# Softmax denominators summed in pairs of key tiles, shift rows by a whole-array transpose, and the batch loop written out

## Chip, cores and metric

One Trainium2 chip, one of its cores. The metric is the device time of one execution in microseconds (us): 2568.3 us as the median of three runs (2564.93 to 2572.62).

## What is computed

Cross-attention followed by a gated feed-forward block, both with a residual. The batch is 16, with 224 queries and 750 keys each, model width 512, 16 heads of 32:

```python
qh, kh, vh = proj(layernorm(x), Wq, bq), proj(ctx, Wk, bk), proj(ctx, Wv, bv)
attn = softmax(einsum('bhqd,bhkd->bhqk', qh, kh) / sqrt(32))
x = x + einsum('bhqk,bhkd->bhqd', attn, vh) @ Wo.T + bo
h = silu(fp4_linear(layernorm(x), w_gate)) * fp4_linear(layernorm(x), w_up)
x = x + fp4_linear(h, w_down)
```

`fp4_linear` rounds input and weight, in blocks of 16, to eight magnitudes with a common scale. The feed-forward width is 1408.

## The kernel before

**Stages.** `attention` runs first (to about 1797 us of the profile), then `feed_forward_weights` splits the rounded weights, then `feed_forward` runs. The change is in `attention` alone.

**Tiling.** Each batch has four slots, one for each group of four heads (`HG`); slot number and group number are the same, and `t` is the number of a group counted over all batches. The 750 keys are six tiles (`KT`) of 125 (`KW`), taken in three pairs `p`. In a slot TensorE makes twelve `score` units (pair p, head j; line 490), each of two key tiles in one bank, and ScalarE takes their exponential into `probs[p]` (line 542). A `pv` unit (line 505) multiplies one pair by the values: eight matmuls, each of 32 output columns, head j in partitions 32j to 32j+31 of `pv_bank[t % 2]`. An fp32 matmul leaves two records in the trace, so a `pv` unit has 16.

**The denominator.** GpSimd adds the six key tiles into one `prob_sum`: one add for pair 0 (line 717) and two chained ones for each of pairs 1 and 2 (line 722), five to a slot. When all five are there, TensorE multiplies the sum with a block of ones (`sum`, line 512, four matmuls, eight records) into the other half of `pv_bank`. VectorE then takes the reciprocal (657) and scales the heads (661), ScalarE and VectorE split the result (584, 665).

**The shift.** For the group one ahead, TensorE makes sixteen `max` units (475) into `max_bank`, VectorE reduces each (617), and after the eighth and the sixteenth negates the maximum into `neg_max` (622). TensorE turns these four columns into rows 96 to 99 of a bank by a matmul with the identity (`shift`, 479), ScalarE copies them into `qstack` (578), where the next group's scores take them up. `max` needs `q_masked`, which SyncE's DMA queue writes from `q_part` (803).

**Other work in the slots.** Projections of keys (429), queries (440), values (449) and the output (465) of this batch or of the one to come. VectorE also rounds a share of the feed-forward weights in slots 0, 1 and 3 (`ffn_quant`, eleven steps in lines 849 to 869; the last is line 869) and SyncE stores it (785). SyncE stacks keys and queries of the next group by DMA (`stack_low` 811, `stack` 817 and 820) and loads the context (788) and x (792) of the next batch in slot 0. GpSimd also adds the output bias to the residual in slot 3 (735).

**Order.** Nothing is planned at run time. Every unit has a place in its slot on a scale on which score i stands at i; `SLOT_PLACES` holds the places by slot, `slot_units` sorts the units by them, and each of the five engines walks through the same list and does its part of each unit, waiting on semaphores. An engine never passes over a unit. `phases` runs batch 0 as written-out code, batches 1 to 14 in one hardware loop (`engine.Fori`, in which the counts waited for are computed in registers), and batch 15 as written-out code again, followed by `END_UNITS`.

## Time and profile before

| | |
|---|---|
| median of three runs | 2568.3 us |
| the profiled execution | 2569.35 us, span of its trace 2567.3 us |
| TensorE matmul busy | 2236.7 us (87%), 15012 records |
| VectorE busy | 2028.4 us (79%) |
| ScalarE busy | 850.8 us (33%) |
| GpSimd busy | 785.2 us (31%) |
| mean granted TensorE clock | 0.93 of full speed |
| GpSimd adds of `prob_sum` (lines 717, 722) | 64 and 256, 694.7 us together |
| `sum` matmuls (line 512) | 512 records, 39.7 us |
| `shift` matmuls (line 479) | 256 records, 45.4 us |

The page's busy shares are averages over stages with different limits. Below, a batch of the loop is followed in the timeline; a row there has start, duration, engine, line, operation, output<-input, the number of merged records, and in brackets how long the engine had been idle before it and what ended the idle time. "PE" is TensorE, "DVE" VectorE, "ACT" ScalarE, "POOL" GpSimd, "SPq" SyncE's DMA queue. "Issue" is idle time that nothing in the profile explains.

### The profile page before, as it was taken

How to read it: one execution, taken by the hardware profiler on the slowest of the kernel's cores; microseconds unless marked ns; L12 is line 12 of the kernel's file. 1: busy time of each engine (PE TensorE's matmuls, PEld its weight loads, DVE VectorE, ACT ScalarE, POOL GpSimd, SP SyncE). 2: the span in 40 equal slices, each digit the busy share in tenths (PEclk: the TensorE clock that was granted, in tenths of full speed). 3: DMA queues.
4: the chain of work that ended last, by engine and by line, in shares of the span. 5: the costliest groups of instructions: out<-in, count | busy, mean ns of one | idle time of the engine just before them, and what ended most of it. 6: DMA issues, size and time to landing. Idle time of an engine off the chain costs nothing. (4 is left out here: it accounts for less than half of the span.)

```text
span 2567.3 us, 46677 instructions
## 1 busy us (share of the span) xinstructions
PE 2236.7 (87%) x15012; PEld 1846.1 (72%) x15012; DVE 2028.4 (79%) x3101; ACT 850.8 (33%) x1677; POOL 785.2 (31%) x484
## 2 busy tenths in 40 slices
PE   4989888798888889888898878887499999999998
PEld 4777667676667667676676667674378888888887
DVE  4878778787877678777787877776689999999986
ACT  3434344343434334343343434333311111111111
POOL 0444444444434434443434434445000000000000
PEclk9989899898989889988998989897799999999999
DMA  4342333433233342333433233332500101101000
GB/s 149 96 118 76 108 84 109 115 78 110 75 108 95 93 111 78 101 86 104 116 77 110 73 106 84 103 85 56 163 22 29 37 25 37 33 28 37 25 25 25
DMA packets 136288, 204.70 MB, mean 80 GB/s; under 512 B 33872, under 2 KB 84560, under 8 KB 133568
## 3 DMA queue, kind: packets, MB, share of 16 engines
q1 hardware_dynamic: 136128, 202.22, 28.1%
q8 instruction: 143, 2.34, 0.4%
q14 instruction: 17, 0.14, 0.0%
HBM read 75.67 MB, written 23.33 MB: 39 GB/s over the span
## 5 line engine op out<-in xcount | busy, mean ns | idle before, releaser
L617 DVE TENSOR_REDUCE row_max<-max_bank 112x1 f32<-112x376 f32 (+1 forms) x1024 | 524.3, 540 | 343.8 <-PE max_bank L475 338.9
L722 POOL TENSOR_TENSOR prob_sum<-prob_sum,probs 125x896 f32<-125x896 f32 x256 | 556.1, 2172 | 491.0 <-ACT probs L542 479.7
L542 ACT ACTIVATE probs<-score_bank 125x448 f32<-125x448 f32 x768 | 405.7, 543 | 379.4 <-PE score_bank L490 374.7
L475 PE MATMUL max_bank<-k_high,q_masked 128*112 128x376 f32 (+1 forms) x1024 | 349.6, 385 | 143.1 <-DVE row_max L617 71.8
L490 PE MATMUL score_bank<-qstack,kstack 100*128 100x224 f32 x1536 | 319.5, 295 | 69.7 <-issue 66.1
L490 PEld LDWEIGHTS score_bank<-qstack,kstack 100*128 100x128 f32 x1536 | 279.8, 203 | 116.7 <-issue 104.0
L475 PEld LDWEIGHTS max_bank<-k_high,q_masked 128*112 128x112 f32 x1024 | 176.5, 190 | 227.7 <-DVE row_max L617 105.0
L717 POOL TENSOR_TENSOR prob_sum<-probs 125x896 f32<-125x896 f32 x64 | 138.6, 2166 | 379.5 <-ACT probs L542 294.8
L449 PE MATMUL proj_bank<-wv_hi,ctx_hi 128*128 128x256 f32 x768 | 226.2, 294 | 4.3 <-DVE wo_lo L696 4.3
L1115 PE MATMUL gate_bank<-ffn_gate_hi,f_xqt 128*128 128x512 f32 (+1 forms) x672 | 218.8, 387 | 8.1 <-DVE f_xqt L1221 8.1
L505 PE MATMUL pv_bank<-probs,values 125*32 125x224 f32 x3072 | 221.7, 411 | 0.0
L449 PE MATMUL proj_bank<-wv_hi,ctx_lo 128*128 128x256 f32 x768 | 220.0, 286 | 0.0
L449 PE MATMUL proj_bank<-wv_lo,ctx_hi 128*128 128x256 f32 x768 | 219.5, 286 | 0.0
L1160 ACT ACTIVATE f_act_gate<-gate_bank 128x512 f32<-128x512 f32 (+1 forms) x84 | 47.3, 563 | 516.4 <-PE up_bank L1115 516.4
L1139 PE MATMUL down_bank<-ffn_down_hi,f_hqt 128*128 128x512 f32 x616 | 207.2, 403 | 6.6 <-DVE f_hqt L1237 6.6
L1115 PE MATMUL up_bank<-ffn_up_hi,f_xqt 128*128 128x512 f32 (+1 forms) x672 | 212.3, 377 | 0.0
L1179 POOL TENSOR_TENSOR f_rstd<-f_mean_var,ln_consts 128x1 f32<-128x1 f32 x28 | 5.4, 192 | 634.8 <-DVE f_mean_var L1196 634.8
L429 PE MATMUL proj_bank<-ctx_hi,wk_hi 128*128 128x376 f32 (+1 forms) x512 | 180.2, 352 | 20.0 <-DVE ctx_lo L651 20.0
L550 ACT ACTIVATE k_high<-proj_bank,biases 128x376 fp32r<-128x376 f32 (+1 forms) x128 | 73.6, 575 | 354.1 <-PE proj_bank L429 354.1
L429 PE MATMUL proj_bank<-ctx_lo,wk_hi 128*128 128x376 f32 (+1 forms) x512 | 177.4, 346 | 0.0
L429 PE MATMUL proj_bank<-ctx_hi,wk_lo 128*128 128x376 f32 (+1 forms) x512 | 175.8, 343 | 0.0
L449 PEld LDWEIGHTS proj_bank<-wv_hi,ctx_hi 128*128 128x128 f32 x768 | 150.6, 196 | 13.6 <-issue 6.1
(120 smaller groups left out, 4523.8 us busy)
## 6 DMA issues: line engine op xcount, KB each, us to landing
kstack<-k_high SPq DMA_DIRECT2D x512, 93.8 KB, 2.2
ctx_raw<-in_ctx SPq DMA_DIRECT2D x16, 1500.0 KB, 7.0
kstack<-k_low SPq DMA_DIRECT2D x256, 93.8 KB, 2.2
qstack<-q_part SPq DMA_DIRECT2D x768, 28.0 KB, 1.8
ffn_quant<-fw_share SPq DMA_DIRECT2D x48, 176.0 KB, 1.8
fw_raw<-ffn_quant SPq DMA_DIRECT2D x33, 256.0 KB, 4.1
xn<-in_x SPq DMA_DIRECT2D x16, 448.0 KB, 8.4
q_masked<-q_part SPq DMA_DIRECT2D x256, 28.0 KB, 1.8
```

Source lines behind the costliest of these rows:

```text
L429: last = nc.tensor.matmul(out[:, 0:hi - lo], w_hi_lo[W_K][ws][:, c, g * P:(g + 1) * P], ctx_part[cs][:, c, lo:hi], start=(n == 0), stop=(n ...
L449: last = nc.tensor.matmul(out[:, 0:256], ctx_part[cs][:, c, kt * KW:kt * KW + P], w_hi_lo[W_V][ws][:, c, half * 256:(half + 1) * 256], sta ...
L475: nc.tensor.matmul(out[0:QH, 0:hi - lo], q_masked[t % 2][:, j, half * QH:(half + 1) * QH], k_part[t % 2][0][:, lo:hi], start=True, stop=Tr ...
L490: last = nc.tensor.matmul(score_bank[j % 2][:, k * SQ:(k + 1) * SQ], kstack[t % 2][0:STK, j, kt * KW:kt * KW + P], qstack[t % 2][:, j, :], ...
L505: last = nc.tensor.matmul(pv_bank[t % 2][j * DK:(j + 1) * DK, 0:SQ], values[:, t % NG // 2, kt, col:col + DK], probs[p][:, j, k, :], start ...
L542: nc.scalar.activation(probs[p][:, j, :, :], score_bank[j % 2][0:KW, 0:2 * SQ].rearrange("p (k q) -> p k q", k=2), ACT.Exp, scale=float(DK ...
L550: nc.scalar.activation(k_part[t % 2][0][:, lo:hi], src[:, 0:hi - lo], ACT.Identity, bias=biases[:, 1, t % NG:t % NG + 1]).then_inc(hi_done ...
L617: nc.vector.tensor_reduce(row_max[:, half, j, kh:kh + 1], mbank[0:QH, 0:KSPLIT[kh + 1] - KSPLIT[kh]], AX.X, ALU.max).then_inc(max_reduced, 1)
L717: nc.gpsimd.tensor_tensor(prob_sum[:, :, :], probs[0][:, :, 0, :], probs[0][:, :, 1, :], ALU.add).then_inc(summed, 1)
L722: nc.gpsimd.tensor_tensor(prob_sum[:, :, :], prob_sum[:, :, :], probs[p][:, :, k, :], ALU.add).then_inc(summed, 1)
L1115: last = nc.tensor.matmul(banks[par][:, 0:w], xqt[n % 2][xs_][:, kc, :], ffn[m][ws][:, kc, chunk(c)], start=(k == 0), stop=(k == 11))
L1139: last = nc.tensor.matmul(down_bank[n % 2][:, :], hqt[hs][:, m, :], ffn[2][ws][:, m, :], start=(m == 0 and k == 0), stop=(m == FC - 1 and ...
```

## The change

- **Pairs.** GpSimd adds only the two key tiles of each pair, into one of two buffers (`pair_sum`): three independent adds to a slot. TensorE multiplies each pair's sum with ones and accumulates the three in the bank: three `sum` units to a slot. The first stands right behind the group's second `pv`, the second right behind its third, the last where the only one stood. GpSimd's add waits for the `sum` two before it, TensorE's `sum` for its add.
- **Loop.** The fourteen batches of the loop are written out, with constants in all waits and addresses.
- **Shift.** `neg_max` is 128 columns wide, zero but for columns 96 to 99; TensorE transposes it over the whole array, and the rows land in the same partitions.

```diff
     add(at["pv"], ("pv", g, 0), ("pv", g, 1))
+    add(at["pv"][1] + 0.01, ("sum", g, 0))
     if not (first and g == 0):
         add(at["pv_last"], ("pv", g - 1, 2))
-        add(at["sum"], ("sum", g - 1))
+        add(at["pv_last"] + 0.01, ("sum", g - 1, 1))
+        add(at["sum"], ("sum", g - 1, 2))
...
-END_UNITS = [("pv", 3, 2), ("sum", 3), ("inverse", 3, 0), ...
+END_UNITS = [("pv", 3, 2), ("sum", 3, 1), ("sum", 3, 2), ("inverse", 3, 0), ...
...
-    prob_sum = sb("prob_sum", [KW, HG, SQ])
+    pair_sum = [sb(f"pair_sum{i}", [KW, HG, SQ]) for i in range(2)]
-    neg_max = sb("neg_max", [QH, 2, HG])
+    neg_max = sb("neg_max", [QH, 2, P])
...
-        body(0, batch_units(True, False), list(v_end), list(m_end))
-        with engine.Fori(1, batches - 1) as b:
-            body(b, batch_units(False, False), list(v_end), list(m_end))
+        for b in range(batches - 1):
+            body(b, batch_units(b == 0, False), list(v_end), list(m_end))
...
-                    nc.tensor.matmul(out[SHIFT:STK, 0:QH], neg_max[:, u[2], :], ident[0:QH, 0:QH],
-                                     start=True, stop=True).then_inc(made["shift"], 1)
+                    nc.tensor.transpose(out[:, 0:QH], neg_max[:, u[2], :],
+                                        ident[0:QH, 0:QH]).then_inc(made["shift"], 1)
...
-                    reached(pe, summed, 5 * (b * NG + t) + 5)
+                    p = u[2]
+                    reached(pe, paired, count(b, *u))
                     for j in range(HG):
                         last = nc.tensor.matmul(pv_bank[t % 2][j * DK:(j + 1) * DK, SQ:2 * SQ], ones[0:KW, :],
-                                                prob_sum[:, j, :], start=True, stop=True)
+                                                pair_sum[index_of(u, b) % 2][:, j, :], start=False, stop=(p == 2),
+                                                skip_group_check=True)
...
-                        reached(act, summed, 5 * (b * NG + t - 1) + 2 * p + 1)
+                        reached(act, paired, count(b, "sum", t - 1, p))
...
                     pool.wait_ge(exp_done, count(b, "score", t, p, HG - 1))
-                    if p == 0:
-                        reached(pool, made["sum"], count(b, "sum", t - 1))
-                        nc.gpsimd.tensor_tensor(prob_sum[:, :, :], probs[0][:, :, 0, :], probs[0][:, :, 1, :],
-                                                ALU.add).then_inc(summed, 1)
-                    else:
-                        for k in range(2):
-                            pool.wait_ge(summed, base + 2 * p - 1 + k)
-                            nc.gpsimd.tensor_tensor(prob_sum[:, :, :], prob_sum[:, :, :], probs[p][:, :, k, :],
-                                                    ALU.add).then_inc(summed, 1)
+                    reached(pool, made["sum"], count(b, "sum", t, p) - 2)
+                    nc.gpsimd.tensor_tensor(pair_sum[index_of(("sum", t, p), b) % 2][:, :, :], probs[p][:, :, 0, :],
+                                            probs[p][:, :, 1, :], ALU.add).then_inc(paired, 1)
```

## Rows read from the trace of the kernel before

**Rows 1.** Stretches view, batches 2 to 13: engines' busy us, granted clock, DMA share.

```profile
267.00:1583.00 1316.00, 1125.00 (x8640) 923.44 (x8639) 1008.66 (x1788) 533.97 (x1080) 569.66 (x312) 0.91 0.36 97
```

**Rows 2.** Waits view, whole span: who waited for whom, total us, times, longest.

```profile
PE max_bank L475 <- DVE row_max L617: 71.8, 53, 5.1
PE max_bank L475 <- DMA q_masked<-q_part: 70.5, 15, 7.8
PE score_bank L490 <- issue: 66.1, 14, 5.4
```

**Rows 3.** Timeline, all engines, around the loop's jump from batch 5 to 6.

```profile
692.98 2.52 POOL L735 TENSOR_TENSOR res<-res,bo_rows 112x512 f32<-112x512 f32 x2 [2.43 <-DMA res<-in_x]
693.05 2.72 DVE L866 TENSOR_SCALAR fw_share<-fw_share 128x352 uint32<-128x352 uint32 x1
...
695.45 4.56 POOL L722 TENSOR_TENSOR prob_sum<-prob_sum,probs 125x896 f32<-125x896 f32 x2
695.81 2.27 DVE L868 SCALAR_TENSOR_TENSOR fw_share<-fw_power,fw_share 128x352 f32<-128x352 f32 x1
698.12 2.28 DVE L869 TENSOR_TENSOR fw_share<-fw_share,fw_scale 128x352 f32<-128x352 f32 x1
699.70 0.76 PE L490 MATMUL score_bank<-qstack,kstack 100*128 100x224 f32 x2 [5.27 <-issue]
...
700.42 0.38 SPq L785 DMA_DIRECT2D ffn_quant<-fw_share  x1
```

**Rows 4.** Timeline at the same place between batches 0 and 1, without a jump.

```profile
154.42 0.96 PE L505 MATMUL pv_bank<-probs,values 125*32 125x224 f32 x16
...
159.37 0.53 DVE L869 TENSOR_TENSOR fw_share<-fw_share,fw_scale 128x352 f32<-128x352 f32 x1
...
160.41 0.66 PE L475 MATMUL max_bank<-k_high,q_masked 128*112 128x376 f32 x1 [5.03 <-DVE row_max L617]
```

**Rows 5.** Timeline, TensorE, start of slot 1 in batch 6.

```profile
729.11 0.97 PE L475 MATMUL max_bank<-k_high,q_masked 128*112 128x376 f32 x2 [4.78 <-DMA q_masked<-q_part]
```

**Rows 6.** Timeline, end of slot 1 in batch 6.

```profile
755.26 4.74 POOL L722 TENSOR_TENSOR prob_sum<-prob_sum,probs 125x896 f32<-125x896 f32 x2 [2.71 <-ACT probs L542]
...
755.60 2.03 DVE L687 TENSOR_SCALAR xn<-xn,mean_var,rstd 112x512 f32<-112x512 f32 x1
...
758.10 2.29 DVE L869 TENSOR_TENSOR fw_share<-fw_share,fw_scale 128x352 f32<-128x352 f32 x1
...
760.90 0.65 PE L475 MATMUL max_bank<-k_high,q_masked 128*112 128x376 f32 x1 [2.96 <-DVE row_max L617]
```

**Rows 7.** Stretches view, right behind that wait (columns as in the first group).

```profile
760.90:767.20 6.30, 6.30 (x41) 4.36 (x41) 4.96 (x8) 3.47 (x7) 0.00 (x0) 0.50 0.51 131
```

**Rows 8.** Timeline, end of batch 2, where the order of the last steps differs.

```profile
372.25 2.28 DVE L869 TENSOR_TENSOR fw_share<-fw_share,fw_scale 128x352 f32<-128x352 f32 x1
```

**Rows 9.** Timeline of SyncE's queue after the two places.

```profile
159.92 0.36 SPq L785 DMA_DIRECT2D ffn_quant<-fw_share  x1
...
163.28 0.35 SPq L781 DMA_DIRECT2D fw_share<-in_gate  x1
...
704.80 0.35 SPq L781 DMA_DIRECT2D fw_share<-in_gate  x1
```

**Rows 10.** Timeline, TensorE: one `pv` unit and one `sum` unit at full clock.

```profile
722.96 0.96 PE L505 MATMUL pv_bank<-probs,values 125*32 125x224 f32 x16
...
738.72 0.58 PE L512 MATMUL pv_bank<-prob_sum,ones 125*32 125x224 f32 x8
```

**Rows 11.** Groups by line and form, TensorE: busy us, mean ns; idle us before, releaser, its us.

```profile
L479 PE MATMUL max_bank<-ident,neg_max 112*4 112x112 f32 x256 | 45.4, 258 | 36.1 <-DVE neg_max L622 36.1
...
L457 PE MATMUL proj_bank<-ident,xn 112*128 112x112 f32 x128 | 23.8, 324 | 0.9 <-DVE k_low L631 0.9
```

**Rows 12.** Timeline, TensorE after the jump into batch 14, and the attention's tail.

```profile
1583.01 0.76 PE L490 MATMUL score_bank<-qstack,kstack 100*128 100x224 f32 x2 [5.30 <-issue]
...
1784.38 0.98 PE L512 MATMUL pv_bank<-prob_sum,ones 125*32 125x224 f32 x8 [4.93 <-POOL prob_sum L722]
```

27 lines of the change are left out of this document (15 added, 12 removed).

## The prediction, made before the changed kernel was run

> **What bounds the kernel now.** I read the stretches first: over batches 2 to 13 TensorE's matmuls are busy 1125 of 1316 us, VectorE 1009, at a granted clock of 0.91 [rows 1]. So neither engine is the bound all the time. The view of waits then says where TensorE stands still: about 5 us in front of the first score of a batch for no visible reason, 14 times and 66.1 us in all; 70.5 us in 15 waits for `q_masked`; and 71.8 us for VectorE's row maxima [rows 2]. The timeline puts these at three places of every batch.
>
> *Place A, the jump.* The first score starts 5.27 us after TensorE's last matmul. But VectorE is late as well: its last `ffn_quant` step runs from 698.12 for 2.28 us, to 700.40, after TensorE is back at 699.70 [rows 3]. Between batches 0 and 1 the code is straight, there is no such gap, and TensorE makes a score, two `max` and a `pv` at once; then it waits 5.03 us for VectorE all the same [rows 4]. The jump hides a wait that is already there.
>
> *Place B, start of slot 1.* TensorE waits 4.78 us for `q_masked` [rows 5]. SyncE's queue issues that DMA as the last of more than thirty, one after the other, and the series begins with the store of line 785, which waits for VectorE's last step (700.40, the store at 700.42) [rows 3]. From there to 729.11 it is 28.7 us whatever TensorE does.
>
> *Place C, end of slot 1.* Again a last `ffn_quant` step takes 2.29 us, and TensorE waits 2.96 us for VectorE [rows 6]. Behind it the granted clock is 0.50, the lower of the two levels, for 6.3 us [rows 7].
>
> From C to the shift of slot 3 TensorE runs nearly without a stop and is the bound. From that shift on, VectorE is.
>
> *Why VectorE is late.* Line 866 takes 2.72 us while GpSimd adds the bias (692.98, 2.52 us), line 868 takes 2.27 us beside GpSimd's first chained add, and line 869 takes 2.28 us beside the second, which ends at 700.01 [rows 3]. The same line 869 takes 0.53 us when GpSimd is still [rows 4]. Each GpSimd add holds up one such step for itself. The Trainium skill, "SBUF — State Buffer", section "Who interferes with whom", says that a VectorE instruction with two SBUF inputs and a GpSimd instruction that reads SBUF fully block each other; by that rule, the trace agrees.
>
> **The change, part by part.**
>
> *GpSimd.* Two adds to a slot go, 128 of 320, about 2.2 us each (4.56 us for two [rows 3]). In most of a slot this costs or gives nothing, as VectorE has room there. At the two places it counts. Place C: GpSimd's pair runs from 755.26 for 4.74 us, and the step at 758.10 meets its second add [rows 6]. Without that add the step takes 0.53 us: 1.76 us earlier, in all 16 batches, 28 us. (The one add that remains now waits for the slot's first `sum`, behind the second `pv`, so it starts later; I estimate 757.4 us, as that `pv` takes 0.96 us and stands behind the shift made from a maximum of just before 755.6. Line 687, from 755.60 for 2.03 us [rows 6], and line 868 would take about 0.55 us each when nothing blocks them, so line 869 is done at about 757.2. It is a margin of a few tenths.) End of slot 3: bias add, then one pair add; lines 866 and 868 are still blocked, 869 is free: 1.8 us. At the end of batch 2 line 868 had already fallen to the bias and 869 to the first add, which stays [rows 8], so there is nothing to gain; three of the fifteen ends look like that. 12 times 1.8 is 22 us. As the DMA series of place B starts from this step, the gain passes on through B undiminished.
>
> *The loop.* TensorE's 5.27 us themselves give nothing, by place A. SyncE gains: from the store to the next load it takes 4.38 us with the jump (700.42 to 704.80) and 3.36 us without (159.92 to 163.28) [rows 3, 9]. That is 1.0 us on the chain that sets place B. A second straight passage (batches 14 to 15) gives 1.3; I take 1.1 for 13 jumps inside the path: 14 us. The Trainium skill, "Runtime: NRT & Kernel Launch", section "Instruction fetch mechanics", says that a taken branch outside the window breaks the sequential prefetch and stalls until the target is fetched. The 5.27 us and the rule fit; what it would be worth if nothing lay underneath is a rival below.
>
> *TensorE's new work.* 128 more `sum` units, four matmuls each. They stand right behind a `pv`, in the same columns. A `pv` unit of 16 records takes 0.96 us and a `sum` of 8 takes 0.58 [rows 10], so eight more records behind others cost 0.38 us; alone it is the full 0.58. I take 0.38, since all the new ones have a `pv` in front. The shift is one record instead of two: 45.4 us by 128 is 0.35 us against 23.8 by 128, 0.19 us, for a whole-array transpose of the same 112 columns [rows 11]; 0.17 us less each. The weight load is wider (128 columns for 4), but loads lie beside matmuls. In slot 0 both vanish in the wait for the DMA at B. In slot 1 they are 0.76 less 0.34, 0.4 us, which the wait at C takes up: 2.96 less 1.76 less 0.4 leaves 0.8 us of it. In slots 2 and 3 they lie on the path: 4 times 0.38 less 4 times 0.17 is 0.8 us to a batch, 13 us.
>
> *The clock.* If the wait at C shrinks from 2.96 to 0.8 us, the stretch at half clock behind it may shorten or go. 6.3 us at 0.50 [rows 7] lose 3.2 us against full clock. The bounds are 0 and 3.2 us a batch. The trace shows no wait of that length alone. I take the middle, 1.6 us, for 15 batches: 24 us. This is the least certain term.
>
> *Waits that are added.* TensorE's `sum` now waits three times to a slot, with scores queued behind it. The first one's add can start when pair 0's exponentials are done, and the `sum` stands behind the `pv` of pair 1, a third of a slot (some 9 us) later, against 2.2 us for the add. The second stands behind the third `pv`, in the next slot, a third of a slot after its own add could start, too. GpSimd's add waits for the `sum` two before it, which has been made everywhere except at C (above). I cost these at nothing. ScalarE's wait for the pair add is likewise met a slot ahead. Zeroing `neg_max` costs one VectorE memset at the start, beside the first loads.
>
> *The tail.* TensorE waits 4.93 us for the last add at 1784.38 [rows 12]. One add of 2.2 us is left out there: 2 us.
>
> **The sum.** Minus 28 (C), minus 22 (end of slot 3), minus 14 (SyncE), minus 24 (clock), plus 13 (TensorE), minus 2 (tail): 77 us, of which the rest of the kernel (feed-forward) sees nothing. The profiled execution has 2569.35 us against a median of 2568.3, 1 us apart, so I take it off the median: 2491 us. A batch, now 110.4 us (699.70 to 1583.01 in 8 batches [rows 3, 12]), would take about 105.5.
>
> **The rivals.**
>
> *1. The locks only move.* The margin at C is a few tenths, and the pair add could start before line 869; then the step is blocked as before, the wait at C stays and with it the half clock. For it: start times shift with the clock, and batch 2 shows that the order differs from batch to batch [rows 8]. Against it: there is one add less to meet. At C alone it takes 28 and some 10 of the 24: about 2528 us. At both places it takes 28, 22 and 24: 2565 us, no change that can be measured.
>
> *2. TensorE eats it.* The new `sum` units cost 0.58 us and more for their semaphores, the shifts save nothing, the clock gives nothing: 24 for the clock, and 4 times 0.58 by 16, 37 us, in place of 13: 2539 us. Against it: the adjacent records in [rows 10].
>
> *3. The jump counts in full.* By the rule on branches, 5.27 us of issue gap go in each of 13 jumps [rows 3]: 69 us instead of 14, so 2436 us. Against it stand the 5.03 us of the straight passage [rows 4] and SyncE's series, which starts from VectorE.
>
> *4. Slower: `sum` waits for its add.* TensorE passes nothing over, so a pair add that isn't done holds up the scores, ScalarE and all behind. The place is the first `sum` of a slot; it decides when GpSimd starts pair 0's add more than 7 us late. The price is one add, 2.1 us, 64 times, 134 us: 2491 plus 134 is 2625 us. Against it: GpSimd is busy 570 of 1316 us [rows 1] and gets less to do.
>
> **How the numbers follow.** My forecast has 0.68. Locks that stay at C have 0.08, at both places 0.08; TensorE eating it 0.07; the jump in full 0.04; slower 0.05. The range starts where the clock gives its upper bound (24 us more) and the loop a little: 2460. It ends past rivals 1 at C and 2, at 2545. That leaves out 0.17. A measurement of this kernel tells some 0.3% (8 us) from no change; faster is all but both-places locks and rival 4, and a little of the former: 0.88; same 0.07; slower 0.05.
>
> **What would show it.** Line 869 in slots 1 and 3 at about 0.5 us. TensorE's gap at the jumps gone, with a wait of about 3 us for VectorE's row maximum in its place. From VectorE's last step in slot 3 to the first `max` of slot 1 about 27.5 us instead of 28.7, with a wait for `q_masked` of 3 us or more still there. The wait at C under 1 us and the 6.3 us at 0.50 behind it shorter. 1536 records for `sum`, 128 for the shift, with the first `sum` 0.4 us long behind its `pv`. The prediction is wrong if line 869 stays at 2.3 us, if `sum` shows idle time that ends with GpSimd's add, or if the wait at B grows by what the others lose.

## Result and profile after

The changed kernel takes 2429.5 us (median of four runs, 2423.72 to 2433.84), beside 2566.6 us for the kernel before on the same chip: a ratio of 0.948 with an interval from 0.942 to 0.954. The forecast was 2491 us with a range from 2460 to 2545. The direction was right, the gain was 137 us instead of 77, and the time lies below the range. One execution of `only_straight`, below, took 11406.8 us for a reason that no run shows; its row goes by its three others.

| | after |
|---|---|
| the profiled execution | 2423.72 us, span of its trace 2421.9 us |
| TensorE matmul busy | 2194.9 us (91%), 15908 records |
| VectorE busy | 1825.4 us (75%) |
| ScalarE busy | 846.4 us (35%) |
| GpSimd busy | 511.4 us (21%) |
| mean granted TensorE clock | 0.96 of full speed |

Batches 2 to 13 in the stretches view (length, busy us of TensorE, its weight loads, VectorE, ScalarE, GpSimd, then granted clock, DMA share and GB/s), to be read beside [rows 1]:

```profile
252.60:1461.90 1209.30, 1091.95 (x9285) 910.85 (x9286) 855.14 (x1788) 529.64 (x1078) 361.87 (x215) 0.95 0.39 105
```

VectorE is busy 154 us less for the same 1788 instructions. None of its work was taken out of these batches, so it had spent that time blocked. GpSimd has 208 us less, TensorE 33 us less in spite of 645 more records, because the clock rose from 0.91 to 0.95.

The view of waits (who waited for whom, total us, times, longest), beside [rows 2]:

```profile
PE max_bank L477 <- DMA q_masked<-q_part: 117.1, 16, 8.9
PE max_bank L477 <- DVE row_max L622: 27.7, 61, 2.5
```

The issue gap before the first score (66.1 us in [rows 2]) is gone, and of the 71.8 us for the row maxima 27.7 are left. The wait for `q_masked` grew from 70.5 to 117.1 us: TensorE comes to place B earlier and waits there longer, as the path from VectorE's last step to that DMA kept its length (first column of the table below).

Groups of VectorE's rounding steps (busy us, mean ns of one, idle time before), before and then after:

```profile
L861 DVE SCALAR_TENSOR_TENSOR fw_power<-fw_share,fw_power 128x352 uint32<-128x352 uint32 x48 | 78.1, 1627 | 0.6
L869 DVE TENSOR_TENSOR fw_share<-fw_share,fw_scale 128x352 f32<-128x352 f32 x48 | 63.8, 1330 | 1.1
L859 DVE TENSOR_SCALAR fw_power<-fw_power 128x352 f32<-128x352 f32 x48 | 45.3, 943 | 0.0
```

```profile
L859 DVE TENSOR_SCALAR fw_power<-fw_power 128x352 f32<-128x352 f32 x48 | 44.2, 922 | 0.0
L869 DVE TENSOR_TENSOR fw_share<-fw_share,fw_scale 128x352 f32<-128x352 f32 x48 | 42.1, 876 | 1.1
L861 DVE SCALAR_TENSOR_TENSOR fw_power<-fw_share,fw_power 128x352 uint32<-128x352 uint32 x48 | 25.9, 539 | 0.6
```

Line 861 is blocked almost nowhere any more, line 869 less often, line 859 as before.

**A batch in four parts.** Everything below is read by cutting the cycle from one end of slot 3 to the next at four marks that a timeline shows: E, the end of VectorE's last rounding step of slot 3 (line 869); the first `max` of slot 1; the first score of slot 2; the first score of slot 3; and E again. The table has the means over batches 1 to 14 in us, worked out from those rows of each kernel's timeline. "Forecast" is what the prediction's terms come to for a batch.

| kernel | E to `max` (jump, place B) | to slot 2 (slot 1) | to slot 3 (place C, slot 2) | to E (slot 3) | sum |
|---|---|---|---|---|---|
| before | 28.21 | 28.14 | 26.80 | 26.55 | 109.70 |
| after | 27.97 | 28.53 | 22.01 | 22.19 | 100.70 |
| after less before | -0.24 | +0.39 | -4.79 | -4.36 | -9.00 |
| forecast | -1.0 | +0.4 | -3.4 | -1.0 | -5.0 |

Place C and slot 2 gained 1.4 us more than forecast, slot 3 gained 3.3 us more, and the jump 0.8 us less.

**Place C.** The timeline of batch 6 (start, duration, engine, line, operation):

```profile
713.09 0.33 DVE L866 TENSOR_SCALAR fw_share<-fw_share 128x352 uint32<-128x352 uint32 x1
...
714.57 0.54 DVE L692 TENSOR_SCALAR xn<-xn,mean_var,rstd 112x512 f32<-112x512 f32 x1
715.02 0.52 DVE L868 SCALAR_TENSOR_TENSOR fw_share<-fw_power,fw_share 128x352 f32<-128x352 f32 x1
...
715.57 0.53 DVE L869 TENSOR_TENSOR fw_share<-fw_share,fw_scale 128x352 f32<-128x352 f32 x1
715.87 0.56 PE L516 MATMUL pv_bank<-pair_sum,ones 125*32 125x224 f32 x8
...
716.61 2.10 POOL L722 TENSOR_TENSOR pair_sum<-probs 125x896 f32<-125x896 f32 x1 [6.59 <-PE pv_bank L516]
```

Line 869 takes 0.53 us instead of 2.29 [rows 6], and GpSimd's add, held by the `sum`, comes only 0.5 us after it: the margin of a few tenths held, in all 16 batches. All of slot 2 in batch 6 in the stretches view (columns as above), before and then after:

```profile
757.11:784.72 27.61, 24.13 (x180) 19.69 (x181) 21.07 (x34) 13.55 (x26) 12.32 (x7) 0.88 0.33 81
```

```profile
716.36:738.36 22.00, 21.53 (x199) 18.41 (x195) 16.40 (x31) 13.23 (x26) 9.01 (x4) 1.00 0.38 94
```

The stretch has no half clock left (1.00 instead of 0.88). In the kernel before, the same stretch has 0.88 in five of the batches 1 to 14 and 0.94 in nine, 0.92 in the mean; in the changed kernel it has 1.00 in all fourteen.

**The end of slot 3.** Here are the two forms that it has in the changed kernel. In batch 4 the bias add catches one step (in [rows 3] it and the two adds behind it caught three):

```profile
556.43 0.53 DVE L868 SCALAR_TENSOR_TENSOR fw_share<-fw_power,fw_share 128x352 f32<-128x352 f32 x1
556.89 2.53 POOL L735 TENSOR_TENSOR res<-res,bo_rows 112x512 f32<-112x512 f32 x2 [5.20 <-DMA res<-in_x]
556.99 2.81 DVE L869 TENSOR_TENSOR fw_share<-fw_share,fw_scale 128x352 f32<-128x352 f32 x1
...
559.38 2.38 POOL L722 TENSOR_TENSOR pair_sum<-probs 125x896 f32<-125x896 f32 x1
```

In batch 6 it comes after all of them:

```profile
758.75 0.53 DVE L869 TENSOR_TENSOR fw_share<-fw_share,fw_scale 128x352 f32<-128x352 f32 x1
759.27 2.52 POOL L735 TENSOR_TENSOR res<-res,bo_rows 112x512 f32<-112x512 f32 x2 [5.81 <-DMA res<-in_x]
759.31 0.35 SPq L785 DMA_DIRECT2D ffn_quant<-fw_share  x1
...
761.75 2.12 POOL L722 TENSOR_TENSOR pair_sum<-probs 125x896 f32<-125x896 f32 x1
```

In the kernel before, the end that has its last three steps free is no free end. This is batch 12:

```profile
1462.87 2.52 POOL L735 TENSOR_TENSOR res<-res,bo_rows 112x512 f32<-112x512 f32 x2 [1.58 <-DMA res<-in_x]
1465.34 4.38 POOL L722 TENSOR_TENSOR prob_sum<-prob_sum,probs 125x896 f32<-125x896 f32 x2
```

```profile
1462.96 4.83 DVE L864 SCALAR_TENSOR_TENSOR fw_share<-fw_power,fw_share 128x352 f32<-128x352 f32 x1
1467.72 2.25 DVE L665 SCALAR_TENSOR_TENSOR o_part<-heads,biases,o_part 128x224 fp32r<-128x224 f32 x1
1469.89 0.33 DVE L866 TENSOR_SCALAR fw_share<-fw_share 128x352 uint32<-128x352 uint32 x1
1470.26 0.52 DVE L868 SCALAR_TENSOR_TENSOR fw_share<-fw_power,fw_share 128x352 f32<-128x352 f32 x1
1470.82 0.52 DVE L869 TENSOR_TENSOR fw_share<-fw_share,fw_scale 128x352 f32<-128x352 f32 x1
```

Lines 864 and 665 took the locks there. GpSimd's three adds stand without a gap, some 7 us in all, and in twelve of the first fifteen ends VectorE's blocked instructions cover all three, whichever instructions these are; in the other three (batch 2 and two more) the third add falls behind VectorE's last step. From ScalarE's copy of the last shift rows before slot 3 to E the kernel before needs 26.4 us three times and 28.2 to 28.6 us twelve times; the changed one needs 21.85 us in eight of the first fifteen batches, 24.1 in six and 25.8 in one. Where no add meets the steps it is 22.4 us with the old shift (`pool_waits_before`, below) and 21.85 with the new, so the locks cost 5.9 or 4.0 us before the change, and 0, 2.2 or 4.0 after it.

### The profile page after: what moved, and what is told of

The parts are those of the page before. It is cut to its first block and busy times, and to the rows that moved or that the text cites. A ratio compares the mean times of both kernels' runs of the same rounds, so it can differ in the third digit from the quotient of the medians.

```text
span 2421.9 us, 42288 instructions
## 1 busy us (share of the span) xinstructions
PE 2194.9 (91%) x15908; PEld 1830.3 (76%) x15908; DVE 1825.4 (75%) x3102; ACT 846.4 (35%) x1677; POOL 511.4 (21%) x356
## 5 line engine op out<-in xcount | busy, mean ns | idle before, releaser
L722 POOL TENSOR_TENSOR pair_sum<-probs 125x896 f32<-125x896 f32 x192 | 419.8, 2186 | 866.2 <-ACT probs L547 759.1
L477 PE MATMUL max_bank<-k_high,q_masked 128*112 128x376 f32 (+1 forms) x1024 | 332.8, 368 | 145.9 <-DMA q_masked<-q_part 117.1
L477 PEld LDWEIGHTS max_bank<-k_high,q_masked 128*112 128x112 f32 x1024 | 166.8, 181 | 223.6 <-issue 151.7
L492 PE MATMUL score_bank<-qstack,kstack 100*128 100x224 f32 x1536 | 299.9, 282 | 3.7 <-ACT probs L547 1.6
L492 PEld LDWEIGHTS score_bank<-qstack,kstack 100*128 100x128 f32 x1536 | 265.3, 192 | 33.5 <-issue 19.1
L507 PE MATMUL pv_bank<-probs,values 125*32 125x224 f32 x3072 | 198.0, 378 | 0.0
L1115 PEld LDWEIGHTS gate_bank<-ffn_gate_hi,f_xqt 128*128 128x128 f32 x672 | 126.3, 189 | 28.0 <-DVE f_xqt L1221 8.5
L451 PEld LDWEIGHTS proj_bank<-wv_lo,ctx_hi 128*128 128x128 f32 x768 | 147.2, 192 | 0.0
```

Source lines behind the costliest of these rows:

```text
L451: last = nc.tensor.matmul(out[:, 0:256], ctx_part[cs][:, c, kt * KW:kt * KW + P], w_hi_lo[W_V][ws][:, c, half * 256:(half + 1) * 256], sta ...
L477: nc.tensor.matmul(out[0:QH, 0:hi - lo], q_masked[t % 2][:, j, half * QH:(half + 1) * QH], k_part[t % 2][0][:, lo:hi], start=True, stop=Tr ...
L492: last = nc.tensor.matmul(score_bank[j % 2][:, k * SQ:(k + 1) * SQ], kstack[t % 2][0:STK, j, kt * KW:kt * KW + P], qstack[t % 2][:, j, :], ...
L507: last = nc.tensor.matmul(pv_bank[t % 2][j * DK:(j + 1) * DK, 0:SQ], values[:, t % NG // 2, kt, col:col + DK], probs[p][:, j, k, :], start ...
L722: nc.gpsimd.tensor_tensor(pair_sum[index_of(("sum", t, p), b) % 2][:, :, :], probs[p][:, :, 0, :], probs[p][:, :, 1, :], ALU.add).then_inc ...
L1115: last = nc.tensor.matmul(banks[par][:, 0:w], xqt[n % 2][xs_][:, kc, :], ffn[m][ws][:, kc, chunk(c)], start=(k == 0), stop=(k == 11))
```

## Experiments

### The change repeated, and each part alone or left out

These show how the three parts share the gain. Straight-line batches alone, and pairs alone, are the kernel before with one part of the diff shown above; so is the shift alone. `loop_kept` is the changed kernel with

```diff
-        for b in range(batches - 1):
-            body(b, batch_units(b == 0, False), list(v_end), list(m_end))
+        body(0, batch_units(True, False), list(v_end), list(m_end))
+        with engine.Fori(1, batches - 1) as b:
+            body(b, batch_units(False, False), list(v_end), list(m_end))
```

`old_shift` is the changed kernel with

```diff
-                    nc.tensor.transpose(out[:, 0:QH], neg_max[:, u[2], :],
-                                        ident[0:QH, 0:QH]).then_inc(made["shift"], 1)
+                    nc.tensor.matmul(out[SHIFT:STK, 0:QH], neg_max[:, u[2], :], ident[0:QH, 0:QH],
+                                     start=True, stop=True).then_inc(made["shift"], 1)
```

with `neg_max` four columns wide again, and `old_sum` is the changed kernel with the five adds and the one `sum` of before.

`only_straight`: 

> The kernel before with the fourteen batches of the loop written out, nothing else. Theory 'locks' (VectorE, held up by GpSimd's adds, is late at the end of slot 3, so the jump hides a wait): TensorE's 5.2 us of issue gap turn into about 5 us of waiting for VectorE, only SyncE's 1 us per jump is won: 2550 to 2560 us, the waits for the row maximum rise from 72 to about 135 us. Theory 'jump' (the gap counts in full, with the half clock behind it): 13 times 5.2 us or more, 2500 us or less.

`only_pairs`: 

> The kernel before with the pair sums alone: three adds a slot on GpSimd, three sum units on TensorE; loop and old shift kept. Theory 'locks': the wait at the end of slot 1 (3 us) and the half clock behind it go, 4.5 us in each of 16 batches, and VectorE is no longer late at the end of slot 3, but the jump now stands bare, so that only 1 to 4 us of that come through: 2430 to 2480 us, issue gap still 66 us. Theory 'jump': pairs bring the smaller part, 2520 us or more.

`loop_kept`: 

> The changed kernel with the loop of batches 1 to 14 put back. Theory 'locks': jump and DMA series overlap (TensorE reaches the wait for q_masked later, but the series on SyncE's queue sets its end), so it costs 1 to 3 us a batch: 2440 to 2475 us, the wait for q_masked falls from 117 us by most of what the issue gap of about 66 us adds. Theory 'jump': 5.2 us and the half clock in 13 batches on top of 2429, 2500 us or more.

`old_shift`: 

> The changed kernel with the shift as a matmul into rows 96 to 99 again. By the term of the prediction 0.17 us each on the path of slots 2 and 3, four a batch: 11 us more, 2435 to 2445 us. A rival, that leaving and entering the column-tiled form on both sides costs TensorE more than the records' busy time says (0.3 us and more each, and a longer way from maximum to qstack): 2450 us or more.

`old_sum`: 

> Straight-line batches and the whole-array shift, with the old denominator (five GpSimd adds, one sum). Straight-line batches alone gave 2525 us. The old shift in the changed kernel cost 24 us (2452 against 2428). If the shift's gain is its own (0.17 us and its waits in each slot), it is there with the old adds too: 2500 to 2510 us. If it needs free VectorE steps (the slots before it end with VectorE either way), it is mostly hidden here: 2515 to 2525 us. A time near 2450 us would say that the locks of the added GpSimd adds were not what the pairs took away.

`only_shift`: 

> The kernel before with nothing changed but the shift (neg_max 128 columns wide, whole-array transpose). In kernels without blocked steps the path from the shift of slot 3 to VectorE's last step is 0.6 us shorter with it (21.84 against 22.41). Here that path is set by GpSimd's adds, and the start of slot 1 by SyncE's series, so a part of 0.3 us for each of two or three slots of a batch is left: 5 to 15 us, 2550 to 2560 us. A gain of 25 us or more, as with the other parts present, would say that the shift's price does not depend on them.

`changed_again`: 

> The changed kernel once more, as the measure for the others of this call: 2425 to 2435 us.

Measured (ratio to the kernel before on the same chip; the parts of a batch as above):

| kernel | median us | ratio, interval | E to `max` | to slot 2 | to slot 3 | to E |
|---|---|---|---|---|---|---|
| only_shift | 2556.9 | 0.998 [0.995, 1.001] | 28.02 | 28.13 | 26.75 | 26.49 |
| only_straight | 2524.1 | 0.982 [0.977, 0.988] | 26.99 | 28.12 | 26.52 | 24.57 |
| only_pairs | 2454.2 | 0.955 [0.950, 0.960] | 29.15 | 28.72 | 22.32 | 23.18 |
| old_sum | 2495.8 | 0.972 [0.966, 0.978] | 27.29 | 28.16 | 26.43 | 23.08 |
| loop_kept | 2452.4 | 0.957 [0.953, 0.962] | 28.04 | 28.55 | 22.06 | 23.28 |
| old_shift | 2452.2 | 0.957 [0.953, 0.961] | 27.61 | 28.54 | 22.31 | 23.80 |
| changed_again | 2428.5 | 0.944 [0.939, 0.950] | 28.31 | 28.47 | 22.01 | 21.96 |

The pairs carry most of it: 109 us alone, 67 us on top of the other two. Place C belongs to them and to nothing else: 26.4 to 26.8 us with the five adds, 22.0 to 22.3 with the three. They also add the 0.4 us in slot 1 that the forecast had for TensorE's new work. The straight code gives 1.2 us at E to `max`, as the forecast had it. Beside the pairs it gives 1.5 us with the old shift (29.15 in `only_pairs`, 27.61 in `old_shift`) and nothing with the new one (28.04 in `loop_kept`, 27.97 and 28.31 without the loop). The shift alone can't be told from no change; with the other two it is worth 24 us, mostly in slot 3, where the parts decide together how many of GpSimd's adds VectorE meets.

Three expectations missed. `only_straight` is faster than its 2550 to 2560 us, and the reason is slot 3, which is 2.0 us shorter though no GpSimd add is gone: from ScalarE's copy to E its first fifteen ends need 28.3 us four times, 26.4 six times, 24.6 four times and 22.4 once, where the kernel before has 28.2 to 28.6 twelve times. That alone is 28 us in 14 batches. `old_shift` is above its 2435 to 2445 us, in the range of its rival, and `old_sum` a little below its 2500 to 2510. In `only_pairs` the time is inside the range, but the gap at the jump is 23.2 us in 11 waits and not the 66 us expected.

### Is it the blocking by GpSimd's reads?

Both kernels start from `old_shift` and give GpSimd work behind its second and third pair add of each slot: two more adds, or five memsets, into a scratch tile that nobody reads.

```diff
+                    if p > 0:
+                        reached(pool, spare, 2 * (b * NG + t) + p - 1)
+                        same = ident[0:KW, :].unsqueeze(1).to_broadcast([KW, 7, P])
+                        nc.gpsimd.tensor_tensor(scratch[:, :, :], same, same, ALU.add).then_inc(spare, 1)
```

```diff
+                    if p > 0:
+                        for n in range(3 if p == 1 else 2):
+                            reached(pool, spare, 5 * (b * NG + t) + 3 * (p - 1) + n)
+                            nc.gpsimd.memset(scratch[:, :, :], 0.0).then_inc(spare, 1)
```

`more_adds`: 

> The changed kernel with the old shift (2452 us measured) and, behind the pair adds of pairs 1 and 2, one more GpSimd add each of the same 125 x 896 size, from the identity tile into a scratch tile: nobody waits for them, TensorE's work is the same, GpSimd is busy as before the change. Theory 'locks': VectorE's steps are held up again, line 869 at 2.3 us in slot 1 with a TensorE wait of 1.5 to 3 us and the half clock behind it, and GpSimd's bias add and last add meet the steps at the end of slot 3: 2500 to 2530 us. Theory 'shorter way of the denominator' (what won was that the sum comes in pieces): 2450 to 2460 us, no change.

`more_memsets`: 

> As the one with two more adds, but with five memsets of the scratch tile in a slot (about 0.84 us each, the same GpSimd time), which write and read nothing. If any busy GpSimd instruction held VectorE up, 2500 to 2530 us. If two-source VectorE steps (lines 868, 869) are held up by GpSimd's reads alone, they stay at 0.53 us and only one-source steps such as line 866 or 687 are longer, by at most the 0.84 us of one memset: 2452 to 2470 us.

Measured: 2541.7 us (ratio 0.989 [0.983, 0.996]) and 2463.3 us (0.958 [0.952, 0.964]), against 2452.2 for `old_shift` (measured on another chip; its ratio is 0.957). The added groups of the two kernels (busy us, mean ns, idle before):

```profile
L729 POOL TENSOR_TENSOR scratch<-ident 125x896 f32<-125x896 f32 x128 | 247.3, 1932 | 0.0
```

```profile
L729 POOL MEMSET scratch<- 125x896 f32 x320 | 273.8, 856 | 11.1
```

247 us of added adds cost 89 us, 274 us of added memsets 11 us (by the ratios, 3.2% and 0.1%). So what counts is not how long GpSimd is busy but that it reads while VectorE does. The adds lengthen the same two parts, slot 2 from 22.31 to 25.62 us and slot 3 from 23.80 to 26.36; with the memsets these are 22.33 and 23.97. In slot 2, though, they do it at another step than I expected: line 869 stays at 0.52 us at the end of slot 1, and the last two of VectorE's four `ctx_lo` steps, which have two inputs in SBUF, take 1.43 and 2.82 us where all take 0.93 in `old_shift`. Batch 6 of `more_adds`:

```profile
763.46 4.17 DVE L658 TENSOR_TENSOR ctx_lo<-ctx_raw,ctx_hi 128x750 fp32r<-128x750 f32 x2
764.56 2.27 POOL L724 TENSOR_TENSOR pair_sum<-probs 125x896 f32<-125x896 f32 x1 [0.47 <-ACT probs L549]
767.78 0.41 PE L433 MATMUL proj_bank<-ctx_hi,wk_hi 128*128 128x376 f32 x1 [2.27 <-DVE ctx_lo L658]
```

A rival, that the added adds only make TensorE's `sum` wait for its pair add, has one wait of 4.3 us in the whole trace. The time is above the 2500 to 2530 us expected. The Trainium skill, "SBUF — State Buffer", section "Who interferes with whom", says that a GpSimd instruction which only writes doesn't contend with a VectorE instruction that has two SBUF inputs; the two runs agree, with 11 us against 89.

### Why did slot 3 gain 4.4 us instead of 1?

My theory after the first runs: the time of GpSimd's bias add is set by the DMA of `res`, which stands in SyncE's queue behind the series that begins with the store of slot 1. In the changed kernel it starts 42.3 to 43.9 us after the start of slot 1's last step, before the change 43.9 to 45.6. Counted from ScalarE's copy of the last shift rows before slot 3, it starts at 20.0 to 21.1 us before the change and at 20.5 to 22.0 after it, while VectorE, when nothing blocks it, is done at 22.4 and at 21.85. So in the changed kernel its last steps can slip in ahead of the add. And since GpSimd passes nothing over, the last pair add stays behind the bias add and is kept off the steps too. The rivals: the slot is shorter because less is queued on GpSimd, wherever the bias add stands, or because TensorE gets through it faster.

`bias_early` lets the DMA of `res` go earlier, so that the bias add falls among the steps in every batch:

```diff
-        "load_res": 6.6,
+        "load_res": 5.9,
```

> The changed kernel with the load of the residual in slot 3 placed in front of the four copies into q_masked on SyncE's queue (place 5.9 for 6.6), so that GpSimd's bias add can start about 3 us earlier. Theory 'the bias add fell behind' (in the changed kernel it starts as VectorE's last step begins or just after it, because SyncE's series of DMAs keeps its length while slots 2 and 3 became shorter): the old order comes back, the bias add holds up one or two of the last steps, VectorE's last step ends 2 to 4 us later in every batch and the DMA series behind it too: 2455 to 2485 us. Rival (VectorE had room there, or the missing second add alone explains it): 2425 to 2440 us.

Measured: 2458.5 us, 0.957 [0.951, 0.964]. Slot 3 to E rose from 22.19 to 24.46 us. As expected.

`bias_next` moves the bias add out of the way, into slot 0 of the next batch:

```diff
     if g == 3:
         add(at["load_res"], ("load_res", 0))
+    if g == 3 and last:
         add(at["add_bias"], ("add_bias", 0))
+    if g == 0 and not first:
+        add(0.17, ("add_bias", -1))
```

> The changed kernel with the bias add moved behind the add of pair 2 at the start of the next batch's slot 0 (the last batch keeps it). Theory: line 869 in slot 3 takes 0.53 us in all batches, where now about eight of fifteen take 2.7 us; 2.2 us less in each of those, passed on by the DMA series: 2405 to 2420 us. Rival (the wait for q_masked is set by something else): no change, 2425 to 2432 us.

Measured: 2448.1 us, 0.955 [0.948, 0.961], slower than the changed kernel: a miss. The timeline of one end:

```profile
660.24 2.21 POOL L725 TENSOR_TENSOR pair_sum<-probs 125x896 f32<-125x896 f32 x1 [4.43 <-PE pv_bank L519]
660.50 2.33 DVE L871 SCALAR_TENSOR_TENSOR fw_share<-fw_power,fw_share 128x352 f32<-128x352 f32 x1
662.41 3.06 POOL L738 TENSOR_TENSOR res<-res,bo_rows 112x512 f32<-112x512 f32 x2
662.87 1.48 DVE L872 TENSOR_TENSOR fw_share<-fw_share,fw_scale 128x352 f32<-128x352 f32 x1
```

Without the bias add ahead of it the pair add starts right among the steps, the bias add follows at once, and 15 of 16 ends lose 2.7 us. I had looked at the bias add as the only thing in the way; it was also the thing that held the pair add back. That is the second half of the theory: with nothing holding the pair add back, it falls among the steps.

`pool_waits` keeps the order, and makes GpSimd wait for VectorE's last step of slot 3 before the bias add. `pool_waits_before` is the same line in the kernel before:

```diff
                     reached(pool, res_loaded, 16 * (b + t + 1))
+                    pool.wait_ge(fw_steps, QSTEPS * (3 * b + 3))
```

`pool_waits`: 

> The changed kernel, in which GpSimd also waits for VectorE's last rounding step of slot 3 before it adds the bias (and so, as it passes nothing over, before its last pair add too). In the trace of the changed kernel about half of the ends of slot 3 have that step blocked for 2.7 us by the bias add, the others don't. Theory (an add that falls among VectorE's steps is paid once, one that falls behind them costs nothing): all ends become free, 2.2 us in each of 8, about 2410 us, with line 869 at about 0.53 us at every end of slot 3. Rival (the free ends are free for another reason, or the later bias add holds up the output's DMA or the last sum): no change or slower, 2428 us or more.

`pool_waits_before`: 

> The same wait in the kernel before: bias add and last chained adds of slot 3 behind VectorE's last step. Theory: the steps of lines 866, 868 and 869 are all free at the end of slot 3, so VectorE gets there some 5 us earlier in a batch; TensorE's gap at the jump of 5.3 us then lies open instead of being hidden, and the sum of the last group comes later, so that of 16 times 5 us, 80 us, part is kept: 2490 to 2515 us. Rival (what VectorE loses to GpSimd at the end of slot 3 is not what sets that slot's length): 2550 us or more.

Measured:

| kernel | median us | ratio, interval | E to `max` | to slot 2 | to slot 3 | to E |
|---|---|---|---|---|---|---|
| pool_waits | 2410.9 | 0.940 [0.934, 0.945] | 27.97 | 28.47 | 22.02 | 20.91 |
| pool_waits_before | 2471.7 | 0.963 [0.957, 0.968] | 29.00 | 26.05 | 26.56 | 21.00 |

In `pool_waits` all the ends are free, as in the timeline of batch 13:

```profile
1441.05 0.52 DVE L870 TENSOR_TENSOR fw_share<-fw_share,fw_scale 128x352 f32<-128x352 f32 x1
1441.60 0.36 SPq L786 DMA_DIRECT2D ffn_quant<-fw_share  x1
1442.00 2.54 POOL L736 TENSOR_TENSOR res<-res,bo_rows 112x512 f32<-112x512 f32 x2 [6.24 <-DVE fw_share L870]
```

Only slot 3 changed, by 1.28 us; times 14 that is 18 us, and the time fell by 18.6 (the intervals of the two ratios overlap, but all four executions, 2410.2 to 2417.4 us, lie below all eight of the changed kernel, 2419.6 to 2433.8). In the kernel before the one wait takes slot 3 from 26.55 to 21.00 us and the time down by 98 us (the median beside it is 2570.1), more than I expected. All that slot 3 gained in the changed kernel, and more, comes without any other part of the change: what it lost before was GpSimd's three adds, 5.55 us of a batch. The changed kernel's 1.28 us is the rest of that. The 98 us are not slot 3 alone (78 us in 14 batches). Slot 1 is 2.1 us shorter too: the wait for `q_masked` ahead of it is nearly gone (5.9 us in two waits), and its granted clock is 1.00 in the mean instead of 0.92; E to `max` takes 0.8 us more. This also leaves no room for the rivals: with as many adds queued as before and nothing changed on TensorE, slot 3 is as short as in `pool_waits`.

### What is the jump worth when nothing covers it?

In `pool_waits_before` VectorE is done early, and TensorE's gap at the jump lies open. One row of its timeline:

```profile
978.88 0.76 PE L490 MATMUL score_bank<-qstack,kstack 100*128 100x224 f32 x2 [5.58 <-DMA kstack<-k_low]
```

The profile names a DMA that landed just then, but the gap has the length of the one in [rows 3], 73.7 us in 13 times, and the DMA copies for the group after this one. So the forecast's third rival, 5.3 us for each jump, could be right here, though it was not for the kernel before. `pool_waits_straight` adds the written-out batches:

> The kernel before with straight-line batches and with GpSimd's bias add behind VectorE's last rounding step of slot 3. With that wait alone (2472 us) TensorE's gap at the jump lies open, 5.6 us in each of 13 batches, and the wait for q_masked is gone. Theory (SyncE's series of DMAs starts from VectorE's last step and takes some 27 us to q_masked without the jump, 28 to 29 with it): removing the jump brings the wait for q_masked back, so a batch gets shorter by about 1.5 to 2.5 us only, 2430 to 2450 us. Rival (the jump counts in full once the locks no longer cover it): 2400 us or less.

Measured: 2461.2 us, 0.962 [0.956, 0.967], above the 2430 to 2450 of the theory and far from the rival's 2400; parts 26.80, 27.27, 26.86, 20.95, sum 101.89 against 102.62. The gap is gone and E to `max` is 2.2 us shorter, as expected, but slot 1 is 1.2 us longer, so 0.73 us of a batch, 10 us in the two traces, are left; by the ratios (0.963 and 0.962) the two kernels can't be told apart. Slot 1 of one batch of each (without the written-out batches, then with them):

```profile
1002.23:1028.16 25.93, 25.22 (x196) 20.91 (x195) 22.22 (x45) 10.28 (x21) 13.70 (x10) 1.00 0.36 95
```

```profile
1406.50:1433.86 27.36, 26.82 (x195) 22.22 (x195) 21.92 (x44) 9.74 (x20) 11.67 (x10) 0.94 0.31 81
```

TensorE is ahead of SyncE's series again, waits for `q_masked` (33.9 us in 15 times), and the granted clock behind that wait is 0.94 instead of 1.00. Another 45.5 us, in 16 waits, are for GpSimd's last `prob_sum`, which stands behind the bias add here, so the edit that uncovers the jump also makes one of the waits that take its place. In this kernel the jump is a delay that two other waits fill; that it would be so in any kernel isn't shown, and with late loads (next section) it is the bound of its part.

### What sets place B?

The series of DMAs from E to the copies into `q_masked` (line 803) has the loads of context (1.5 MB) and x (0.45 MB) ahead of those copies. Batch 7 of the changed kernel:

```profile
776.67 0.58 SPq L788 DMA_DIRECT2D ctx_raw<-in_ctx  x1
777.29 0.43 SPq L792 DMA_DIRECT2D xn<-in_x  x1
777.83 2.47 SPq L803 DMA_DIRECT2D q_masked<-q_part  x4
...
786.40 0.94 PE L477 MATMUL max_bank<-k_high,q_masked 128*112 128x376 f32 x2 [6.71 <-DMA q_masked<-q_part]
```

The copies are issued by 780.30 and TensorE goes on at 786.40, 6.1 us later. The loads can stand behind the copies:

```diff
-        "load": 2.6,
+        "load": 7.3,
```

`load_late`: 

> The changed kernel with the loads of the next batch's context and x placed behind the copies into q_masked on SyncE's queue (place 7.3 for 2.6 in slot 0). Leaves nothing out. Theory (TensorE's wait at the start of slot 1 is the landing of q_masked behind 1.5 MB of context): the copies land about 4 us after they are issued in place of 9, so that the wait of 7.9 us falls to about 2 us and with it the clock's fall: 5.5 us and up to 3 us of clock in each of 14 batches, 2310 to 2360 us. Rival (SyncE's series of DMAs alone sets the time, or the next thing is late by as much): 2400 to 2430 us.

`load_late_before`: 

> The kernel before with the loads of context and x behind the copies into q_masked. Theory (q_masked lands late behind the context in both kernels, but here TensorE has only 4.8 us to win before its own work of slot 0 is the bound, and VectorE stays late at both other places): 3 to 5 us and the shorter half clock in 14 batches: 2490 to 2525 us. Rival (in the kernel before the wait hid VectorE's lateness): 2550 us or more.

`bias_next_load_late`: 

> The changed kernel with both edits. Loads behind q_masked alone gave 2355 us. There the last step was still held up in five of fifteen batches, and TensorE, no longer covered by the wait for q_masked, should feel it in full: 2 to 4 us each: 2340 to 2350 us. If the order falls out as well without it, 2350 to 2360 us.

`pool_waits_load_late`: 

> The changed kernel with both: the loads of context and x placed behind the copies into q_masked (2355 us by itself), and GpSimd's bias add behind VectorE's last step of slot 3. In the kernel with late loads alone three of fifteen ends of slot 3 still had that step blocked. Theory: 2.2 us in each of those, 2340 to 2350 us. Rival (the wait moves the last pair add and sum into the way of slot 0): 2355 us or more.

Measured:

| kernel | median us | ratio, interval | E to `max` | to slot 2 | to slot 3 | to E |
|---|---|---|---|---|---|---|
| load_late | 2355.4 | 0.917 [0.912, 0.922] | 21.41 | 30.07 | 22.00 | 21.78 |
| load_late_before | 2508.8 | 0.979 [0.971, 0.986] | 23.93 | 28.75 | 26.60 | 25.85 |
| bias_next_load_late | 2377.4 | 0.926 [0.920, 0.933] | 21.23 | 30.07 | 22.01 | 23.66 |
| pool_waits_load_late | 2343.6 | 0.912 [0.906, 0.917] | 21.55 | 30.04 | 22.03 | 20.93 |

The same place in the timeline of `load_late`:

```profile
743.05 2.43 SPq L803 DMA_DIRECT2D q_masked<-q_part  x4
745.52 0.58 SPq L788 DMA_DIRECT2D ctx_raw<-in_ctx  x1
...
746.84 0.56 PE L477 MATMUL max_bank<-k_high,q_masked 128*112 128x376 f32 x2 [1.82 <-DMA q_masked<-q_part]
```

TensorE goes on 1.4 us after the last copy is issued. E to `max` falls by 6.6 us in the changed kernel and by 4.3 in the one before, where the jump's gap stays (69.5 us in 13 times): there it becomes the bound of that part. Slot 1 takes 1.5 us more, and the trace shows what the edit costs there: x, whose load moved too, now lands late for the layernorm of the next batch. VectorE's `stats` (line 677) waits for it 90.4 us in 15 times, 6.0 us of each slot 1, and TensorE's waits for VectorE's row maxima in that slot grow from 0.2 to 2.1 us. No run here moves the context alone. The last of the four, with both edits, is the fastest version: 2343.6 us, 86 us below the changed kernel, and near what its expectation said. `bias_next_load_late` missed for the same reason as `bias_next`.

## Why the forecast was wrong, step by step

**Place C, lock: right.** 1.76 us a batch was the forecast; line 869 takes 0.52 or 0.53 us there in all 16 batches.

**Place C, waits and clock: both somewhat too small.** The two parts around C together went from 54.94 to 50.54 us, 4.40 less, where I had 3.0. TensorE's waits for VectorE in slot 2 fell from 3.6 to 0.5 us in the mean of batches 1 to 14, 3.1 less, where the forecast has 1.76 for the lock and 0.4 taken up by TensorE's new work; half a microsecond of it was a wait for the maxima of the shift, which I hadn't counted. The granted clock of slot 2 went from 0.92 to 1.00 in the mean; of 26.8 us that is 2.1 us, where I had 1.6, half of the 3.2 us of batch 6. That batch was one of the five with 0.88, so the upper bound came from the worse kind. 1.4 us more in 14 batches is 20 us of the miss. No run takes the wait away and leaves the lock, so that the clock rose because the wait went is argued and not shown; that slot 2 runs at 1.00 is.

**End of slot 3: the step that failed.** I wrote "lines 866 and 868 are still blocked, 869 is free: 1.8 us", in 12 of 15 ends. That step let one add go and held the times of all others fixed. But the add's time and the steps' time hang on different things, a DMA there and TensorE's pace here, and a change in slots 2 and 3 moves one against the other. Half of the ends became free altogether. The twelve ends weren't alike either. I had read three blocked steps off one of them; in nine line 869 was free already, with lines such as 864 and 665 held by the adds in its place and the slot as long as in the others. So the sign that I had named for slot 3, line 869 at 0.5 us, says nothing: it stood there in nine of the first fifteen ends before the change and in eight after it. The three ends at which I expected no gain were read rightly. Measured: 4.36 us a batch, where the forecast's terms make 1.0. The 3.3 us in 14 batches are 46 us of the miss.

**SyncE and the jump: the series as forecast, the landing not.** 1.0 us a batch was the forecast for E to `max`, 0.24 came (0.10 the other way in the repeated run, 28.31 against 28.21). In the traces SyncE's series itself did get shorter by what I had: from E to the end of the issue of the last copy into `q_masked` it is 22.0 us before, 20.9 and 21.2 in the two runs of the changed kernel. But the copies land 6.9 and 7.0 us after that instead of 6.2, so "the gain passes on through B undiminished" failed. In the means over batches 1 to 14 this landing takes 6.1 to 6.4 us in `only_straight`, `old_sum` and `only_shift`, and 6.7 to 7.0 in `only_pairs`, `loop_kept` and `old_shift`; single batches differ by as much. In all it is 11 us the other way. The wait for VectorE's row maximum of about 3 us, which I had named as a sign, didn't come at the jump (0.6 us in the mean before `max`), and the wait at B grew, which I had named as a sign of being wrong. The third rival (2436 us) comes close to the time by accident: it has 69 us for the jump, where writing out the loop alone takes off 39 us (2563.2 to 2524.1), 28 of them in slot 3, and 10 us with the gap open.

**TensorE's new work: right.** Lines 507 and 516 stand in the timeline of batch 4 like this:

```profile
554.65 0.96 PE L507 MATMUL pv_bank<-probs,values 125*32 125x224 f32 x16
...
555.43 0.56 PE L516 MATMUL pv_bank<-pair_sum,ones 125*32 125x224 f32 x8
```

The `sum` ends 0.38 us after the `pv`, as assumed. The one record of the shift takes 285 ns, not 190:

```profile
L481 PE MATMUL max_bank<-ident,neg_max 112*128 112x112 f32 x128 | 36.5, 285 | 1.2 <-DVE neg_max L627 1.2
```

By records that saves 0.07 us each; yet where all ends are free, the path from ScalarE's copy of the last shift rows before slot 3 to E is 22.41 us with the old shift (`pool_waits_before`) and 21.84 with the new (`pool_waits`), 0.57 less. Neither the loop nor the pairs explain it: `pool_waits_straight` has 22.36 with the old shift, and the free ends of `old_sum` have 21.85 with the new one and the old adds. TensorE shows where a part of it goes: from the start of that shift to the first score of slot 3, with the same value projections between them, it takes 1.80 us with the old shift and 1.54 with the new, 0.26 less for one shift. So by the path a shift saves more than the 0.17 us that I had, and by its own record less.

**The sum.** The two traces lie 145 us apart (2567.3 and 2421.9), 8 more than the medians, so it is 68 us that have to be found. Batches 1 to 14 gained 4.0 us each beyond the forecast, 56 us: 46 in slot 3 and 20 around C, less 11 from E to `max`. Batch 0 gained 8.5 us (E at 159.90 and 151.38) and all behind the E of batch 14 gained 10.9, where I had 2 and 5: 12 us more.

**Rivals 1, 2 and 4** had nothing: no lock at C, TensorE's new work as small as said, and `sum` waits for GpSimd's add for 1.2 us in all (the group below). Why the range missed: its lower end took the clock's upper bound and a little of the loop, and had nothing for slot 3, since I had costed that as if it could only be a lock more or less.

```profile
L516 PE MATMUL pv_bank<-pair_sum,ones 125*32 125x224 f32 x1536 | 116.2, 376 | 1.2 <-POOL pair_sum L722 1.2
```

**What stays open.** Why the copies land later in the kernels with pairs; why `loop_kept` has SyncE's shorter series though it has the loop; and why a shift costs TensorE 0.26 us less when its record is only 0.07 us shorter. At the jump itself the gap isn't always there: `loop_kept` shows 12.9 us of it in 5 waits, `only_pairs` 23.2 us in 11, [rows 2] 66.1 us in 14.

## What to carry to other kernels

When two engines lock each other out, don't price the one pair of instructions that meets in the trace: price the whole series that stands without a gap on the locking engine, and ask what sets its start and what sets the start of the work it blocks. If these are different things, a change anywhere else slides one past the other, and the range must hold "all of it is met" and "none is met". Such a meeting is then worth an edit of its own: one wait that puts the off-path engine behind the critical one took 98 us off the kernel before, more than half of what the whole change took, and 19 us off the changed one. And before a wait for a small DMA is called fixed, look at what large transfer is queued right ahead of it: moving two loads behind it took 73 us, even with VectorE then waiting 6.0 us a batch for the second of them.

## What the runs showed of the hardware

- A VectorE instruction with one input is blocked too: the `TENSOR_SCALAR` on f32 of line 859, which takes 0.33 us when free, starts 0.23 us after a GpSimd add and ends 0.2 us behind it.

```profile
707.88 2.13 POOL L722 TENSOR_TENSOR pair_sum<-probs 125x896 f32<-125x896 f32 x1 [6.59 <-ACT probs L547]
708.11 2.10 DVE L859 TENSOR_SCALAR fw_power<-fw_power 128x352 f32<-128x352 f32 x1
```

  The Trainium skill, "SBUF — State Buffer", section "Who interferes with whom", lists `tensor_scalar` among the operations whose fast mode takes the shared ports; the row agrees.
- Four small copies of 28 KB land 6.1 us after their issue when loads of 1.5 and 0.45 MB were issued from 1.2 us ahead of them on, and 1.4 us after it when the loads are behind them.
- A wait of 2.96 us for VectorE had a stretch at the lower clock behind it, and the waits of 0.5 us in the mean that are left in slot 2 of the changed kernel had none: at place C the granted clock went from 0.50 in 6.3 us [rows 7] to 1.00 in all of slot 2.
